# Two tiles of every 93 fetched row by row by SyncE and ScalarE, beside GpSimd's gathers

## The reference

```python
def _conv(x, row, col, edge_type, edge_weight, W, b):
    ...
    norm = deg_inv_sqrt[row] * deg_inv_sqrt[col] * edge_weight
    xw = jnp.einsum('ni,tio->tno', x, W)
    x_j = xw[edge_type, col] * norm[:, None]
    out = jax.ops.segment_sum(x_j, row, num_segments=N) + b
    return jax.nn.leaky_relu(out, negative_slope=NEG_SLOPE)
...
z1 = _conv(x, row, col, edge_type, edge_attr, W1, b1)
z2 = _conv(z1, row, col, edge_type, edge_attr, W2, b2)
z3 = _conv(z2, row, col, edge_type, edge_attr, W3, b3)
return (x + z1 + z2 + z3) / 4
```

## Time and profile before

| | |
|---|---|
| median of 3 runs | 8947.23 us (8946.75 to 8949.12) |
| the profiled execution's own time | 8944.74 us |
| its span, first to last instruction | 8942.5 us |
| mean granted TensorE clock | 0.619 of full |
| GpSimd's gathers in the layers | 4743 with `rec_idx` and 93 with `first_idx` (the first 31 tiles of each layer) |

### The profile page before, as it was taken

One profiled execution on the slowest core, in us unless ns is written; L12 is line 12 of the kernel. 1 busy time (PEld: TensorE's weight loads), 2 busy tenths in 40 slices (PEclk: granted clock), 3 DMA queues, 4 the chain that ended last, 5 costly groups with the idle time before them and its releaser, 6 DMA issues.

```text
span 8942.5 us, 151268 instructions
## 1 busy us (share of the span) xinstructions
PE 5975.2 (67%) x30961; PEld 4629.3 (52%) x30962; DVE 5414.9 (61%) x15776; ACT 2172.1 (24%) x6655; POOL 6393.3 (71%) x6521
## 2 busy tenths in 40 slices
PE   4886565656666565655657565665656878888886
PEld 4664444444444444444444444444444777777776
DVE  9996444444445444444445444444446888888888
ACT  6550000000001000000001000000003888888887
POOL 0667777777776777777776777777775777777775
PEclk9995555555556555555556555555555887888887
DMA  1002122212224222212123222222222444444443
GB/s 51 35 35 56 53 53 53 53 53 53 53 63 97 53 53 53 53 53 53 53 53 103 53 53 53 53 53 53 53 53 68 115 116 114 116 115 115 115 115 98
DMA packets 432687, 612.45 MB, mean 68 GB/s; under 512 B 232038, under 2 KB 249491, under 8 KB 432539
## 3 DMA queue, kind: packets, MB, share of 16 engines
q0 software_dynamic: 208832, 428.96, 19.0%
q1 hardware_dynamic: 223707, 182.02, 6.5%
HBM read 437.29 MB, written 51.28 MB: 55 GB/s over the span
## 4 chain that ended last, share of the span: by engine, by line
POOL 42%; issue 32%; DMA 9%; DVE 7%; PE 6%; ACT 2%; POOLq 1%; DVEq 1%; SPq 0%; ACTq 0%
POOL g_rows L733 33%; POOL a_roll L758 9%; DMA g_rows<-gcn_table,rec_idx 7%; ACT a_cand L899 2%; DMA a_rows<-a_roll 1%; POOLq L754 1%; PE bank L1161 1%; DVE lo_hot L1227 1%; DVE v_hot L1352 1%; PE wide L1161 1%; PE wide L1044 1%; PE wide L1122 1%; PE wide L1179 0%; DMA a_roll<-gat_table,src_plane 0%; DVE p_hot L1227 0%
## 5 line engine op out<-in xcount | busy, mean ns | idle before, releaser
L733 POOL DMA_INDIRECT g_rows<-gcn_table,rec_idx x4743 | 4487.0, 946 | 1445.8 <-issue 1358.9
L1161 PE MATMUL bank<-g_rows,g_hot 128*128 x7440 | 1906.6, 437 | 1097.5 <-POOLq L710 1037.8
L1161 PEld LDWEIGHTS bank<-g_rows,g_hot 128*128 128x128 f32 x7440 | 1638.5, 324 | 1552.5 <-issue 1550.7
L1604 DVE TENSOR_TENSOR acc<-acc,bank 128x512 f32 x930 | 639.6, 688 | 2092.9 <-PE bank L1161 2090.1
L1589 DVE TENSOR_SCALAR g_hot<-bank,rec_lo,rec_w 128x128 f32<-128x128 f32 x5580 | 1897.3, 402 | 2.2 <-DVE mv L1647 2.0
L758 POOL DMA_INDIRECT a_roll<-gat_table,src_plane x1612 | 1521.2, 944 | 494.6 <-issue 470.0
L1161 PE MATMUL wide<-g_rows,g_hot 128*128 x3720 | 952.4, 437 | 598.0 <-POOLq L710 579.7
L1161 PEld LDWEIGHTS wide<-g_rows,g_hot 128*128 128x128 f32 x3720 | 818.5, 323 | 826.1 <-issue 824.8
L899 ACT ACTIVATE a_cand<-a_miss,a_rows 128x128 f32<-128x128 bf16 x3608 | 1100.2, 387 | 302.2 <-DMA a_rows<-a_roll 299.2
L862 ACT ACTIVATE rows<-bank,inv_deg 128x512 f32<-128x512 f32 x34 | 23.4, 688 | 3914.9 <-PE bank L1122 3914.9
L1604 DVE TENSOR_TENSOR acc<-acc,wide 128x512 f32 x465 | 319.8, 688 | 1063.5 <-PE wide L1161 1062.6
(11 more groups left out here) (268 smaller groups left out, 5604.7 us busy)
## 6 DMA issues: line engine op xcount, KB each, us to landing
a_rows<-a_roll SPq DMA_DIRECT2D x451, 264.0 KB
g_rows<-gcn_table,rec_idx POOLq DMA_INDIRECT x4743
gcn_table<-rows SPq DMA_DIRECT2D x147, 256.0 KB
a_roll<-gat_table,src_plane POOLq DMA_INDIRECT x1612
e_dst<-by_dst_dst SPq DMA_DIRECT2D x451, 2.0 KB
gat_table<-acc SPq DMA_DIRECT2D x7, 462.0 KB
out_x<-xs SPq DMA_DIRECT2D x6, 448.0 KB
gcn_slots<-nothing SPq DMA_DIRECT2D x4, 468.0 KB, 6.8
```

The lines of the kernel that those rows point to most:

```text
L733: pool.indirect_dma_start(out=g_rows[:, tile % RING, :], out_offset=None, in_=gcn_tables[layer % 2], in_offset=bass.IndirectOffsetOnAxis(a ...
L1161: last = nc.tensor.matmul(sums_of(j)[:, bass.ds(place, D)], g_hot[:, j % 3, k, :], g_rows[:, bass.ds(slot, 1), :].rearrange("p g d -> p (g ...
L1604: V.tensor_tensor(dst_ap, dst_ap, sums_of(j).rearrange("p (k d) -> p k d", k=GP), ALU.add).then_inc(s_gadd, 1)
```

## The change

Two columns of the ring, 20 and 66 of 93 (`ROW_COLS`), are taken out of GpSimd's program in turns 1 to 16 of each layer (2 to 16 in the first layer). The tile of column 20 is fetched by SyncE and that of column 66 by ScalarE, as 128 transfers of one row each: the row's number is loaded from `rec_idx` in SBUF into a register, and a DMA from that register's address brings the row into one partition. In odd turns the two tiles lie in two new slots behind the ring (`ring_slot`), so that a fetch does not have to wait until TensorE has read the tile of the turn before. A fetch starts when `s_land` says that the tile one turn earlier in the same column has landed. GpSimd no longer issues these tiles; at their place in `pass_landed` it waits for the rows' own semaphore (`s_row_by`, 16 per row) besides the gathers'. `list_tiles` gets five more operations in each of its four calls, for the two new slots.

```diff
+ROW_COLS = (20, 66)
+ROW_ROUNDS = 16
+ROW_SEMS = 4
...
+def ring_slot(tile):
+
+    turn, at = divmod(tile, RING)
+    return RING + ROW_COLS.index(at) if at in ROW_COLS and turn % 2 else at
+
+
+def row_rounds(layer):
+
+    return range(1 if layer else 2, ROW_ROUNDS + 1)
...
+            def fetch_rows(layer):
+
+                sp.wait_ge(s_idx, CH)
+                for turn in row_rounds(layer):
+                    tile = turn * RING + ROW_COLS[0]
+                    sp.wait_ge(s_land, CH * CCOLS * layer + tile - RING + 1)
+                    for p in range(P):
+                        _, (row,) = nc.values_load_multi_w_load_instructions(
+                            rec_idx[p:p + 1, tile:tile + 1].bitcast(I32), engines=(mybir.EngineType.SP,),
+                            min_val=0, max_val=NB * P * N_TYPES - 1,
+                            skip_runtime_bounds_check_because="a row of the table: a node of a block, and its type")
+                        sp.dma_start(g_rows[p:p + 1, ring_slot(tile), :], gcn_tables[layer % 2][bass.ds(row, 1), :]
+                                     ).then_inc(s_row_by[0][turn % ROW_SEMS], 16)
+
+            fetch_rows(0)
             write_table(1, gcn_wide[1])
...
+            fetch_rows(1)
             write_table(2, gcn_wide[0])
+            fetch_rows(2)
...
             def pass_landed(layer, n):
 
                 q, u = divmod(n, len(FOURS))
                 tiles_n = len(FOURS[u])
-                pool.wait_ge(s_g[u], 16 * tiles_n * (SORT.steps * layer + q + 1))
+                apart = 0
+                for t in FOURS[u]:
+                    tile = TURN * q + t
+                    if by_rows(layer, tile):
+                        turn, at = divmod(tile, RING)
+                        wait_apart(pool, s_row_by[ROW_COLS.index(at)][turn % ROW_SEMS], row_landed(layer, turn), s_apart)
+                        apart += 1
+                if apart < tiles_n:
+                    pool.wait_ge(s_g[u], 16 * gathered(layer, q, u))
                 pool.sem_inc(s_land, tiles_n)
...
+                            if not by_rows(layer, tile):
+                                pool.indirect_dma_start(
...
             for layer in range(3):
+                fetch_rows(layer)
                 end_layer(layer)
...
+                chain(V.tensor_scalar(turn, turn, 1, None, ALU.bitwise_and))
+                for e, col in enumerate(ROW_COLS):
+                    chain(V.scalar_tensor_tensor(row, at, float(col), turn, ALU.is_equal, ALU.mult))
+                    chain(V.scalar_tensor_tensor(at, row, float(RING + e - col), at, ALU.mult, ALU.add))
```

More of the change, by code:

```diff
@@ L96, with by_rows @@
 ROLL = 8
+def ring_slot(tile):
[3 more added lines that the diff above has]
+    return range(1 if layer else 2, ROW_ROUNDS + 1)
+def by_rows(layer, tile):
+    turn, at = divmod(tile, RING)
+    return at in ROW_COLS and turn in row_rounds(layer)
 GAT_GROUPS = EDGES_PAD // (GAT.tiles * P)
@@ L317, in gnn_kernel @@
         rec_w = sb("rec_w", [P, SLOT_TILES], F32, gcn_scope)
-        g_rows = sb("g_rows", [P, RING, D], F32, gcn_scope)
+        g_rows = sb("g_rows", [P, RING + len(ROW_COLS), D], F32, gcn_scope)
         listing = ExitStack()
@@ L397, in gnn_kernel @@
         s_apart = sem("s_apart")
+        s_row_by = [[sem(f"s_row{e}_{k}") for k in range(ROW_SEMS)] for e in range(len(ROW_COLS))]
         s_fin, s_last, s_out = sem("s_fin"), sem("s_last"), sem("s_out")
@@ L442, in of_block, with row_landed @@
             return q.i is not None or 0 <= q.base + lag < NB
+        def row_landed(layer, turn):
+            done = [t for l in range(layer + 1) for t in row_rounds(l)
+                    if t % ROW_SEMS == turn % ROW_SEMS and (l < layer or t <= turn)]
+            return 16 * P * len(done)
         block = ctx.enter_context(nc.Block())
@@ L703, in _, with gathered @@
                 pool.sem_inc(s_paired, 1)
+            def gathered(layer, q, u):
+                return sum(not by_rows(l, TURN * r + t) for l in range(layer + 1)
+                           for r in range(SORT.steps if l < layer else q + 1) for t in FOURS[u])
             def pass_landed(layer, n):
@@ L732, in _ @@
                             at = rec_idx[:, tile:tile + 1] if q else first_idx[:, t:t + 1]
[L733 to L736, removed]
+                            if not by_rows(layer, tile):
+                                pool.indirect_dma_start(
+                                    out=g_rows[:, ring_slot(tile), :], out_offset=None, in_=gcn_tables[layer % 2],
+                                    in_offset=bass.IndirectOffsetOnAxis(ap=at, axis=0),
+                                ).then_inc(s_g[t // 4], 16)
                             n = q * len(FOURS) + t // 4
@@ L749, in rolled @@
             def rolled(g):
-                return 3 * 16 * SORT.steps * len(FOURS[g % ROLL]) + 16 * T * (g // ROLL + 1)
+                return 16 * gathered(2, SORT.steps - 1, g % ROLL) + 16 * T * (g // ROLL + 1)
             for g in range(GAT_GROUPS):
@@ L878, in end_layer, with fetch_rows @@
                         last.then_inc(s_added, 1)
+            def fetch_rows(layer):
+                act.wait_ge(s_idx, CH)
+                for turn in row_rounds(layer):
+                    tile = turn * RING + ROW_COLS[1]
+                    act.wait_ge(s_land, CH * CCOLS * layer + tile - RING + 1)
+                    for p in range(P):
+                        _, (row,) = nc.values_load_multi_w_load_instructions(
+                            rec_idx[p:p + 1, tile:tile + 1].bitcast(I32), engines=(mybir.EngineType.Activation,),
+                            min_val=0, max_val=NB * P * N_TYPES - 1,
+                            skip_runtime_bounds_check_because="a row of the table: a node of a block, and its type")
+                        act.dma_start(g_rows[p:p + 1, ring_slot(tile), :], gcn_tables[layer % 2][bass.ds(row, 1), :]
+                                     ).then_inc(s_row_by[1][turn % ROW_SEMS], 16)
             for layer in range(3):
+                fetch_rows(layer)
                 end_layer(layer)
@@ L1145, in places_of @@
                         gcn_at[32:33, bass.ds(q.at(0), 1), :].rearrange("p g k -> p (g k)"),
-                        engines=(mybir.EngineType.PE,), min_val=0, max_val=(RING - 1) * GP * D,
+                        engines=(mybir.EngineType.PE,), min_val=0, max_val=(RING + len(ROW_COLS) - 1) * GP * D,
                         skip_runtime_bounds_check_because="a slot of the ring, and a block less its group's first")
```

## The result

The changed kernel takes 10302.06 us (median of 5 runs, 10298.48 to 10308.71), the one before 8947.23 us: a ratio of 1.1514, 95% interval 1.1501 to 1.1526. It is 1355 us slower, where 117 us less were forecast, and lies outside the range.

What follows compares the result with a forecast made beforehand. GpSimd's gathers were taken to bound the kernel: 8944.7 us less 117 us for 94 tiles, with no waits for rows, gives 8827, and 8830 us as median; range 8815 to 9150 us for 8 in 10.

Steps and rivals of the forecast that it cites:

- What bounds, and what GpSimd saves: GpSimd's gathers bound the layers at 1.248 us per tile; 94 tiles taken off save 117 us; new waits cost nothing.
- Whether it fits: Per turn, the longer of GpSimd's 113.6 us and 128 x 0.86 + 2.0 = 112.1 us of rows; GpSimd doesn't wait.
- The price of a row: Register load, register operation and DMA per row on SyncE, priced from `e_dst` transfers: 0.855 us, say 0.86; ScalarE the same.
- the same ends: Range for the price of a row: 0.77 to 1.00 us on SyncE, taken over for ScalarE.
- The checks: Two checks behind the register load of `e_dst` transfers, dropped by the change: 0.12 to 0.20 us, taken as 0.18.
- The first: Rival: a row takes longer than a turn allows; 9300 us at 0.95 us per row, 9600 at 1.00; chance 0.27.
- the second: Rival: SyncE and ScalarE share a descriptor generator, about 10440 us, or ScalarE issues more slowly; chance of either 0.09.
- The sign named for it: In GpSimd's gathers: if only ScalarE's column shows gaps, the issuer was mis-priced; no size given.
- The estimate of 0.98 us per row: Row price using the skill's load floor: 0.60 + 0.10 + 0.28 = 0.98 us, the kernel about 9480 us.
- The rest: VectorE's 20 added operations in `list_tiles`, 12.4 us in all, covered by other work or made up by TensorE: taken as 0.

Runs made afterwards that it cites:

- fixed rows: Changed kernel without loading row numbers: each of the 128 DMAs brings a constant table row, on both engines; 8836.58 us, ratio 0.9876.
- four loads: Changed kernel with the same instructions reordered on both engines: four register loads, then their four DMAs; 8833.33 us, ratio 0.9876.
- between: Changed kernel, but SyncE writes each row as 128 single values into 128 partitions and ScalarE copies a value between DMA and next load; 10322.43 us (one run).

## Why the prediction was wrong

**What bounds, and what GpSimd saves: right.** With rows that are in time the kernel gains 110 us (fixed rows) and 112 us (four loads) of the 117 summed. The new waits on GpSimd cost nothing of their own, and TensorE could use the earlier tiles.

**Whether it fits: the rule was right, but for one row.** The longer of GpSimd's 113.6 us and 128 rows with a tail of 2 us, 60 us lost per 0.01 us above 0.872: it names the right stop, and what one turn costs. Its count is one row too long: the tail of 1.95 us runs from the last row's start, so a turn is 127 rows and the tail. So counted, with the measured prices, it gives each of the six runs with rows too slow to within 25 us, five of them to within 8; with 128 rows and 2.0 us it is 46 to 63 us too long.

**The price of a row: the step that failed.** "A row is 0.755 - 0.18 + 0.28 = 0.855 us", and for ScalarE "I take SyncE's price and the same ends". The sum rested on the gap behind an `e_dst` transfer. That transfer has 128 pieces, and behind such a DMA a load takes 0.26 us; behind a row's single piece it takes 0.50. They were the wrong neighbours: the prediction corrected for the pieces in the DMA's own time (0.28 for 0.35, measured 0.255), and not in that of the load behind it. The `between` run has the shape of the earlier trace rows and gives 0.824 us, within 4% of the 0.855, but by two errors that offset each other: without the DMA its row is 0.824 - 0.333 = 0.49 us where the prediction had 0.755 - 0.18 = 0.575, and its DMA is 0.333 and not 0.28 us. The checks were worth more than 0.18. In the trace before, the two (in the first eight rows of this shape) come to 0.26 us with their gaps:

```profile
L534 SPq FUSED_REGOPS  x1: 152/152/152, 6864.7 to 6864.7; - x1
L534 SPq SEQ_ASSERT  x1: 18/18/18, 6864.9 to 6864.9; - x1
```

For SyncE the errors of the price are thus +0.23 us for the load, -0.08 for the checks and -0.03 for the DMA, 0.12 in all. Its 0.978 us still lay within the ends, in part by luck.

ScalarE's 1.127 us did not, and it set the time. Its load is no dearer than SyncE's (0.479); its DMA is, 0.446 where it is the first behind a load, against 0.213 behind another DMA. No row before showed ScalarE issuing, and its ends were borrowed from SyncE. That was the place for a wider range: with both engines at SyncE's 0.978 us the kernel would have taken 8947 + 475 = 9422 us, outside it too.

The prediction also said that "only the sum of load, checks and operation is measured". The trace had the load by itself, at 0.257 us. Using it would have made a row of 0.74 us and a surer forecast in the wrong direction, since nearly all of those loads stand in another order. The loop's first one, at 0.508 us, was the warning.

**The rivals.** The first had the right mechanism and place, with a row of 0.95 to 1.00 us where ScalarE needed 1.127. Of the second, the generator is ruled out as a cause (0.006 us per row); its remark that ScalarE "may also simply be slower than SyncE" was what happened, though as a matter of order. That its 10440 us came near the 10302 is luck: it reckoned with a wait that does not occur. The sign named for it, gaps at ScalarE's column alone, is nearly what the trace shows: SyncE's tiles were in time only because ScalarE's held GpSimd up.

The Trainium skill (DMA: Bandwidth & Descriptors, Latency and other measured facts) has about 600 ns as the floor of a register load. The runs show medians of 0.26 to 0.57 us for one number, so the measurement decides. The estimate of 0.98 us per row that was made from it meets SyncE's 0.978 by luck, with parts that are not so: its load is shorter, and the register operations and gaps around it are 0.20 us, not 0.10. The Trainium skill's sentence on the shared generator (Perfetto Trace Analysis, DMA Instruction — HWDGE) is not borne out here as a delay: ScalarE's DMA has a median of 0.446 us with SyncE's stream and without.

**The rest: taken at 0, right.** The 12.4 us in `list_tiles` came as 12.3 us at TensorE's start, and the ring hid all or most of them.

**What stays open:** why a load is short close behind another, why a DMA of one piece between them undoes that and one of 128 pieces does not, and why ScalarE's first DMA behind a load costs twice the next. The runs show on what they depend, not what goes on inside. `between` changed the number of pieces and the number of partitions written together, so which of the two counts is open too.

## What to carry to other kernels

An instruction on a queue has no price of its own: read it off a row with the same neighbours, of the same shape, on the same engine, and where there is none, widen the range by what the order may do. Where a loop alternates between register loads and small DMAs, group them: the same instructions in fours took 14% less time here (8833 against 10302 us) than one load and one DMA in turn. And work handed to an idle queue has a due time: reckon how often it comes against how long it takes, and look at what stands ahead of its first piece.

## What the runs showed of the hardware that was not expected

- A load of one number (medians): 0.26 to 0.29 us right behind another load, or behind a DMA of 128 pieces with another load shortly before; 0.48 to 0.57 us right behind a DMA of a single row; 0.44 to 0.51 us as the engine's first or behind a pause of 9 us or more (SyncE and ScalarE). Eight numbers in one load behind a DMA of a single row: 0.78 us on SyncE, 0.83 on ScalarE.
- A DMA of one row at a register's address on ScalarE: 0.446 us as the first behind a load, 0.213 us behind another DMA; on SyncE 0.26 and 0.225 us.
- DMAs of single rows at fixed addresses follow each other every 0.295 us on either engine. At about one row per microsecond on each, the two engines slow each other by 0.006 us per row at most.
